# Cross-attention, first batch: a two-tile root, another order of loads, and the turned rows scaled on ScalarE

## The chip, the cores and the metric

The kernel runs on one core of one Trainium2 chip. The metric is the time of one launch on the device, in microseconds (us). The kernel before took 1183.37 us (median of three runs, 1183.1 to 1183.62).

## What is computed

Eight batches of 512 rows with 512 features go through two blocks. The first is a gated cross-attention against a context of the same shape, the second a self-attention with experts. The change touches only the first block, and of it only the first batch.

```python
def _L0_xattn_ref(encoder_hc, decoder_hq, w_sim, b_sim, W_qv, b_qv):
    d = encoder_hc.shape[-1]
    w1, w2, w3 = (w_sim[:d], w_sim[d:2 * d], w_sim[2 * d:])
    Sim = (encoder_hc @ w1)[:, :, None] + (decoder_hq @ w2)[:, None, :] + jnp.einsum('bid,bjd->bij', encoder_hc * w3, decoder_hq) + b_sim[0]
    A = jax.nn.softmax(Sim, axis=2)
    hq_hat = jnp.einsum('bij,bjd->bid', A, decoder_hq)
    Batt = jax.nn.softmax(jnp.max(Sim, axis=2), axis=1)
    hc_bar = jnp.einsum('bi,bid->bd', Batt, encoder_hc)[:, None, :]
    hc_hat = jnp.broadcast_to(hc_bar, encoder_hc.shape)
    feats = jnp.concatenate([encoder_hc, hq_hat, encoder_hc * hq_hat, encoder_hc * hc_hat], axis=-1)
    return feats @ W_qv + b_qv

x = x + jnp.tanh(g_xattn[0]) * _L0_xattn_ref(_layernorm(x, axis=-1), ctx_1024, ...)
x = x + jnp.tanh(g_ffn[0]) * _L0_ffn_ref(_layernorm(x, axis=-1), ...)
```

`_layernorm` subtracts the mean of a row and divides by the root of its variance plus 1e-5. `encoder_hc` is the normalised x, `decoder_hq` the context.

## The kernel before, in words

A batch is four row tiles of 128 rows; its context is held as four tiles of rows (ctx) and four tiles of features (ctx^T, laid out by the host). Every fp32 operand of a product is split in a high part (ScalarE, a copy that rounds, names with `_hi`) and a low part (the rest; VectorE or GpSimd, names with `_lo`), and a product is three passes over four feature tiles, 12 matmuls of 512 columns. The order of work on each engine is written out by hand; semaphores tie the engines together, and each engine works through its own list in order.

What happens in the first batch, before any product can run:

- SyncE (SP) issues the loads in order: four tiles of x (`load_x`), the columns of w_sim (`w_cols`), four tiles of ctx^T (`load_first_ctx_t`), four of ctx (`load_first_ctx`), a weight block `wh_raw`. Then x of batch 1 into the slots of `stage` that the turned rows set free.
- VectorE (DVE) takes the statistics of the four row tiles (`row_stats`, L640), computes 1 over the root of all four variances together in a chain of 17 tiny instructions (`root`, in 14 parts of `mean_rstd`, L47 to L71; each part waits for the one before), and then goes through `first_softmax` (L753 to L798): it normalises the row tiles (L651), takes low parts of ctx^T (`ctx_t_lo`, L253), scales the turned rows with w3 and adds w2 (`first_scaled`, L681: four instructions of 128x128 from PSUM into `tmp`), takes the low part of the scaled rows (`first_scaled_lo`, L689), finds row maxima of the scores (`row_max`, L729), inverts the sums (L734) and takes low parts of the turned probabilities (`probs_lo`, L744).
- TensorE (PE) fills time with transposes of the identity (`fill`, L953), turns the normalised rows (`turn_e`, four transposes, L964), computes the scores of one row tile at a time (`scores`, L946; row tile t waits for `es_lo` t+1), sums the rows against w1 (`first_dots`, L970), turns the probabilities (`turn_a`, L999) and then, when the low part of the last turned probabilities is there, computes the attended context (`attend`, L946 into ps_h). From there on it goes on with the products of the batch (`feats`) and with batch 1.
- ScalarE (ACT) takes the high parts (`ctx_t_hi` and `ctx_hi` and `weights_hi`, all L249; `first_scaled_hi`, L472), copies the turned rows from PSUM (`copy_e`, L466), computes the exponentials (`softmax_exp`, L504), normalises them (`normalise`, L513) and takes the high part of the turned probabilities (`probs_hi`, L509).
- GpSimd (POOL) takes the low parts of ctx and of the weights; it waits for the low parts of the third and fourth scaled row tile first.

Row tile t has t as its number in what follows, so the scores of tile 0 are the first.

Of the kernel before, what the change touches and what calls it, by code (L numbers as in the profile page):

```python
# [24 lines left out]
ALU = mybir.AluOpType  # L25
# [87 lines left out]
def cross_attention(nc, block, both, x, ctx, ctx_t, g_xattn, w_sim, w_sim_cols, b_sim, w_qv, b_qv, x1, w_vsd, wq, wk):  # L113
# [7 lines left out]
    with ExitStack() as mem:  # L121
# [78 lines left out]
        c_lo = sem("c_lo")  # L200
        stats_done = sem("stats_done")
        newton = sem("newton")
        all_stats_done = sem("all_stats_done")
        x1_newton = sem("x1_newton")
        e_ready = sem("e_ready")
# [72 lines left out]

        @block.sync
        def _(sp):  # L280
            def load_x(b, first=False, second=False):
                for t in range(NT):
                    if second:

                        sp.wait_ge(et_ps, t + 1)
                    elif not first:

                        sp.wait_ge(c_lo, b * NT - NT + t + 1)
                    sp.dma_start(stage[:, t, :], of(x_dram, b)[:, t, :]).then_inc(slot_loaded[t], 16)
# [11 lines left out]
                    sp.wait_ge(ct_lo, b * ND + t + 1)  # L301
                    sp.dma_start(stage[:, t, :], of(c_dram, b)[:, t, :]).then_inc(slot_loaded[t], 16)

            def load_first_ctx_t():
                for k in range(ND):
                    sp.dma_start(x_sb[:, k, :], of(ct_dram, 0)[:, k, :]).then_inc(ct0_loaded[k], 16)

            def load_first_ctx():
# [22 lines left out]
                sp.wait_ge(x1_stats_done, (b + 1) * NT)  # L331
                load_residual(b + 1)

            load_x(0, True)
            sp.dma_start(w_cols[:], w_sim_cols).then_inc(cols_loaded, 16)
            load_first_ctx_t()
            load_first_ctx()
            sp.dma_start(wh_raw[:], w_blocks[1]).then_inc(wh_loaded, 16)
            load_x(1, second=True)
# [122 lines left out]
        def _(act):  # L462
            def copy_e(b, t, first=False):
# [2 lines left out]
                act.activation(e_t[:, :, t * P:(t + 1) * P], first_turned[t] if first else turned_e[t],  # L466
                               ACT.Copy).then_inc(et_copied, 1)

            def first_scaled_hi(t):
                cols = slice(t * P, (t + 1) * P)  # L470
                act.wait_ge(es_ready, t + 1)
                act.activation(es_t2[:, 0, :, cols], tmp[:, :, cols], ACT.Copy).then_inc(es_hi, 1)  # L472
# [99 lines left out]
                ctx_hi(b, False)  # L572

            def first_softmax():
                for k in range(ND):
                    ctx_t_hi(0, k, True)
                first_scaled_hi(0)
                copy_e(0, 0, True)
                ctx_hi(0, True)
                first_scaled_hi(1)  # L580
                copy_e(0, 1, True)
                weights_hi(wh, wh_raw, wh_loaded, (0,))
                softmax_exp(0, 0)
                first_scaled_hi(2)
                normalise(0, 0)
                copy_e(0, 2, True)
                softmax_exp(0, 1)
                probs_hi(0, 0)
                first_scaled_hi(3)
                normalise(0, 1)  # L590
                copy_e(0, 3, True)
                weights_hi(wh, wh_raw, wh_loaded, (1,))
                probs_hi(0, 1)
                softmax_exp(0, 2)
                normalise(0, 2)
                weights_hi(wh, wh_raw, wh_loaded, (2, 3))
                probs_hi(0, 2)
                softmax_exp(0, 3)
                normalise(0, 3)
# [34 lines left out]
        def _(dve):  # L634
# [7 lines left out]
            def root(b, part):  # L642
                if part == 0:
                    dve.wait_ge(stats_done, b * NT + NT)
                mean_rstd(dve, part, stats[:], D, mean[:], work[:], rstd[:], newton, b * ROOT_STEPS)

            def normalise_x(b, t):
                if t == 0:

                    dve.wait_ge(newton, b * ROOT_STEPS + ROOT_STEPS)  # L650
                dve.tensor_scalar(e_sb[:, t, :], e_sb[:, t, :], mean[:, t:t + 1], rstd[:, t:t + 1],  # L651
                                  ALU.subtract, ALU.mult).then_inc(e_ready, 1)
# [19 lines left out]
            def scaled_e_lo(b, k):  # L672
                dve.wait_ge(es_hi, b * ND + k + 1)
                take_lo(dve, es_t2, k, tmp).then_inc(es_lo, 1)

            def first_scaled(t):
                dve.wait_ge(et_ps, t + 1)
                if t == 0:
                    dve.wait_ge(cols_loaded, 16)
                for k in range(ND):  # L680
                    last = dve.tensor_scalar(tmp[:, k, t * P:(t + 1) * P], first_turned[t][:, k, :], w3_col[:, k:k + 1],  # L681
                                             w2_col[:, k:k + 1], ALU.mult, ALU.add)
                last.then_inc(es_ready, 1)

            def first_scaled_lo(t):
                cols = slice(t * P, (t + 1) * P)
# [65 lines left out]

            def first_softmax():  # L753

                normalise_x(0, 0)
                normalise_x(0, 1)
                ctx_t_lo(0, 0, True)
                first_scaled(0)
                ctx_t_lo(0, 1, True)
                normalise_x(0, 2)  # L760
                first_scaled_lo(0)
                ctx_t_lo(0, 2, True)
                ctx_t_lo(0, 3, True)
                first_scaled(1)
                normalise_x(0, 3)
                first_scaled_lo(1)
                row_max(0, 0)
                first_scaled(2)
                invert(0, 0)
                first_scaled_lo(2)  # L770
                row_max(0, 1)
                first_scaled(3)
                invert(0, 1)
                probs_lo(0, 0)
                first_scaled_lo(3)
                row_max(0, 2)
                row_stats(1, 0)
                invert(0, 2)
                probs_lo(0, 1)
                row_stats(1, 1)  # L780
                row_max(0, 3)
                row_stats(1, 2)
                invert(0, 3)
                probs_lo(0, 2)
                row_stats(1, 3)
                for part in range(5):
                    root(1, part)
                probs_lo(0, 3)
                first_dots()
                row_totals(0)  # L790
                for part in range(5, ROOT_PARTS):
                    root(1, part)

                first_row_lo(1, 1)
                first_row_lo(2, 2)
# [101 lines left out]
                dve.tensor_scalar(all_stats[:, bass.ds(b * NT, NT), :], x1_stats[:], 1.0, None,  # L897
                                  ALU.mult).then_inc(all_stats_done, 1)

            for t in range(NT):  # L900
                row_stats(0, t, True)
            for part in range(ROOT_PARTS):
                root(0, part)
            first_softmax()
            attended(0, True, True)
            with dve.Fori(0, B - 2) as b:
# [28 lines left out]
        def _(pe):  # L935
# [130 lines left out]
            def softmax(b, first):  # L1066


                scores(b, 0, first)
                if first:  # L1070
                    turn_e(0, 2, True)
                    turn_e(0, 3, True)
                if not first:
                    scores(b, 1, False)
                    feats(b - 1, *LAST_FEATS[0])
# [11 lines left out]
                for t in range(NT):  # L1087
                    if t + 1 < NT:
                        scores(b, t + 1, True)
                    if t == 0:  # L1090
                        first_dots(0)
                    if t == NT - 1:
                        fill(3)
                        first_dots(1)
                        fill(3)
                        first_dots(2)
                        fill(3)
                    turn_a(b, t, True)
                fill(6)
                first_dots(NT - 1)  # L1100

            pe.wait_ge(stats_done, 3)
            fill(18)
            turn_e(0, 0, True)
            turn_e(0, 1, True)
            fill(12)
            softmax(0, True)
            first_feats(0, True, True)
            softmax(1, False)
# [1163 lines left out]
```

## Time and profile before

| | us |
|---|---|
| median of three runs | 1183.37 |
| the profiled execution's own time | 1182.84 |
| its span, first to last instruction | 1181.0 |
| PE busy | 1166.8 (99%) |
| DVE busy | 831.3 (70%) |
| ACT busy | 647.1 (55%) |
| POOL busy | 657.4 (56%) |

The granted TensorE clock is in the highest tenth in all 40 slices of the page. The 1.84 us between the span and the time of that execution lie before the first and behind the last instruction. A row of the timeline gives the start, the length of the merged row, engine, line, operation, what is written from what, and how many instructions it merges; in brackets how long the engine was idle before it and what ended that. Instructions of DVE and ACT overlap a little: a 128x512 copy on ACT lasts 0.62 us, and the next begins 0.52 us after it.

### The profile page before, as it was taken

The page shows a single profiled execution, that of the slowest core. Times are in us where ns is not written, and L with a number is a line of the kernel's source. Part 1 is how long each engine was busy: PE and PEld are TensorE (multiplying, and loading weights), DVE is VectorE, ACT ScalarE, POOL GpSimd, SP SyncE. Part 2 cuts the span into 40 slices and gives each one's busy share as a digit, 9 for nine tenths or more (in the row PEclk, how much of TensorE's full clock was granted, in tenths as well). Part 3 has the DMA queues.
Part 4 walks back from the last instruction along what each step waited for, and adds up shares of the span by engine and source line. Part 5 has one row for each costly group of instructions (what it writes and reads, how often), then busy time and mean ns, then how long its engine had stood idle before and what let it go on. Part 6 is the DMA issues. An engine that isn't in the chain of part 4 may idle for free.

```text
span 1181.0 us, 19684 instructions
## 1 busy us (share of the span) xinstructions
PE 1166.8 (99%) x6377; PEld 910.1 (77%) x6377; DVE 831.3 (70%) x1518; ACT 647.1 (55%) x1444; POOL 657.4 (56%) x476
## 2 busy tenths in 40 slices
PE   7999999999999999999999999999999999999998
PEld 6888888888888888877767777677677777777765
DVE  7888787878787857465675765666666765765868
ACT  6534343434343534477656666556657666665654
POOL 2625242424242425449298297397397396495594
PEclk9999999999999999999999999999999999999999
DMA  5441413131323224401003002002002011010020
GB/s 198 142 134 45 134 55 123 63 114 68 110 77 101 80 62 150 153 11 37 1 1 107 0 18 89 0 27 80 0 36 71 0 60 46 0 71 0 0 72 36
DMA packets 40749, 75.92 MB, mean 64 GB/s; under 512 B 3728, under 2 KB 4240, under 8 KB 40720
## 3 DMA queue, kind: packets, MB, share of 16 engines
q1 hardware_dynamic: 40720, 75.55, 19.1%
q8 instruction: 16, 0.26, 0.1%
q14 instruction: 13, 0.11, 0.0%
HBM read 58.76 MB, written 16.78 MB: 64 GB/s over the span
## 4 chain that ended last, share of the span: by engine, by line
PE 90%; DVE 4%; issue 1%; ACT 0%; POOL 0%; DVEq 0%
PE ps_f L946 21%; PE ps_r L2019 14%; PE ps_o L2089 9%; PE ps_s L2076 8%; PE ps_s L2068 8%; PE ps_s L946 6%; PE ps_h L946 6%; PE ps_r L2028 6%; PE ps_r L2052 4%; PE ps_r L2034 1%; PE ps_r L2010 1%; PE ps_r L2042 1%; DVE nmax L1692 1%; PE ps_t L999 1%; PE ps_h L999 1%
## 5 line engine op out<-in xcount | busy, mean ns | idle before, releaser
L1692 DVE TENSOR_REDUCE nmax<-ps_s 128x1 f32<-128x512 f32 x256 | 158.7, 682 | 112.9 <-PE ps_s L2068 111.9
L1523 ACT ACTIVATE tmp<-ps_s,nmax 128x512 f32<-128x512 f32 x256 | 172.7, 687 | 94.0 <-DVE nmax L1692 94.0
L1466 POOL TENSOR_TENSOR z<-z,z_tmp 128x1280 f32<-128x1280 f32 x35 | 102.9, 2939 | 166.3 <-DVE z_tmp L1706 164.0
L1448 POOL TENSOR_TENSOR spare<-xv,pick 128x512 f32<-128x512 f32 x160 | 169.4, 1059 | 35.6 <-DVE pick L1801 22.7
L1454 POOL TENSOR_TENSOR spare<-spare 128x512 f32<-128x512 f32 x128 | 181.5, 1418 | 10.0
L1532 ACT ACTIVATE pt<-ps_s 128x512 f32<-128x512 f32 x256 | 132.1, 612 | 10.5 <-PE ps_s L2076 10.5
L2076 PE MATMUL ps_s<-ident,tmp 128*128 128x128 f32 x1024 | 122.3, 273 | 0.0
L2076 PEld LDWEIGHTS ps_s<-ident,tmp 128*128 128x128 f32 x1024 | 115.4, 140 | 8.6 <-issue 1.6
L2089 PE MATMUL ps_o<-pt,spare 128*64 128x512 f32 x496 | 113.3, 598 | 0.0
L253 POOL TENSOR_TENSOR e_t<-e_t 128x512 fp32r<-128x512 f32 x28 | 35.4, 1300 | 139.7 <-ACT e_t L493 139.7
L2068 PE MATMUL ps_s<-k,q 64*128 64x512 f32 x768 | 107.0, 409 | 0.1
L2068 PEld LDWEIGHTS ps_s<-k,q 64*128 64x128 f32 x768 | 66.9, 184 | 47.1 <-issue 33.9
L253 POOL TENSOR_TENSOR c<-stage,c 128x512 fp32r<-128x512 f32 x28 | 42.3, 1542 | 97.7 <-ACT c L249 97.7
L2019 PE MATMUL ps_r<-es_t,c_t 128*128 128x512 f32 x384 | 96.2, 399 | 0.0
L2019 PE MATMUL ps_r<-es_t,wk 128*128 128x512 f32 x384 | 95.1, 396 | 0.0
L946 PE MATMUL ps_s<-c_t,es_t 128*128 128x512 f32 x384 | 92.5, 392 | 1.2 <-DVE es_t L689 1.1
L946 PE MATMUL ps_f<-wec,e_t 128*128 128x512 f32 x384 | 92.1, 392 | 0.0
L946 PE MATMUL ps_f<-weh,eh_t 128*128 128x512 f32 x384 | 91.9, 391 | 0.0
L946 PE MATMUL ps_f<-wh,h_t 128*128 128x512 f32 x384 | 91.1, 390 | 0.3 <-DVE x_sb L888 0.3
L946 PE MATMUL ps_h<-es_t,c 128*128 128x512 f32 x384 | 88.7, 390 | 0.0
L946 PEld LDWEIGHTS ps_f<-wh,h_t 128*128 128x128 f32 x384 | 72.0, 188 | 15.6 <-DVE x_sb L888 0.7
L946 PEld LDWEIGHTS ps_s<-c_t,es_t 128*128 128x128 f32 x384 | 71.3, 188 | 16.1 <-DVE es_t L689 1.6
(234 smaller groups left out, 2116.7 us busy)
## 6 DMA issues: line engine op xcount, KB each, us to landing
stage<-in_x SPq DMA_DIRECT2D x32, 256.0 KB, 3.2
x_sb<-in_x SPq DMA_DIRECT2D x8, 1024.0 KB, 5.1
x_dram<-x_sb SPq DMA_DIRECT2D x32, 256.0 KB, 3.3
stage<-x_dram SPq DMA_DIRECT2D x8, 1024.0 KB, 5.7
x_sb<-x_dram SPq DMA_DIRECT2D x8, 1024.0 KB, 5.6
out_dram<-x_sb SPq DMA_DIRECT2D x32, 256.0 KB, 2.0
stage<-in_ctx_t SPq DMA_DIRECT2D x28, 256.0 KB, 2.8
stage<-in_ctx SPq DMA_DIRECT2D x28, 256.0 KB, 2.7
```

The lines of the kernel that those rows point to most:

```text
L253: return eng.tensor_tensor(pair[:, 1, k, :], operand[:, k, :], pair[:, 0, k, :].bitcast(F32), ALU.subtract)
L946: last = pe.matmul(out, left(l, k), right(r, k), start=start and n == 1, stop=stop and n == ND * len(PASSES))
L1448: pool.tensor_tensor(v_tmp[:] if e else acc, xv[:, :, e, :].unsqueeze(2).broadcast_to(shape), pick[:, 0, e, :, 2 * p:2 * p + 2].unsqueeze( ...
L1454: pool.tensor_tensor(acc, acc, v_tmp[:], ALU.add).then_inc(v_steps, 1)
L1466: pool.tensor_tensor(zv, zv, z_tmp[:, h % 2], ALU.add).then_inc(z_pool, 1)
L1523: act.activation(probs[:, n % BANKS, :], ps_s[:, n % BANKS, :], ACT.Exp, bias=nmax[:, n:n + 1], accum_out=den[:, h, t:t + 1]).then_inc(p_e ...
L1532: act.activation(pt[:, h % 4, :, t * P:(t + 1) * P], ps_s[:, n % BANKS, :].rearrange("p (k t) -> p k t", k=NT), ACT.Copy).then_inc(pt_read ...
L1692: dve.tensor_reduce(nmax[:, n:n + 1], ps_s[:, n % BANKS, :], AX_X, ALU.max, negate=True).then_inc(nmax_ready, 1)
L2019: end = pe.matmul(ps, w2[:, l, k, n * P:(n + 1) * P], y_t2[:, r, k, :], start=m == 0, stop=m == len(every) - 1)
L2068: end = pe.matmul(ps_s[:, (n + a) % BANKS, :], q2[head_rows(a), p % 2, l, t * P:(t + 1) * P], k2[head_rows(a), p % 2, r, :], start=m == 0, ...
L2076: end = pe.transpose(ps_s[:, n % BANKS, k * P:(k + 1) * P], probs[:, n % BANKS, k * P:(k + 1) * P], ident[:])
L2089: end = pe.matmul(ps_o[head_rows(a), :], v_acc[:, p, k, a, :], pt[:, p % 2 * 2 + a, k, :], start=k == 0, stop=k == NT - 1)
```

## The change

In `cross_attention`, first batch alone:

- VectorE no longer takes the statistics of all four row tiles before one root. It takes those of tiles 0 and 1, computes their root (`first_root(0, ...)`, a semaphore of its own), normalises both, and then takes the statistics of tiles 2 and 3. Their root's parts are spread between its later work, and `first_normalise(2)` and `(3)` come after the first row maximum.
- SyncE loads x 0 and 1, ctx^T 0 and 1, `w_cols`, x 2 and 3, ctx^T 2 and 3.
- The scaling of the turned rows (`first_scaled`, 16 instructions of 128x128) goes from VectorE to ScalarE, as an activation Identity with a scale and a bias from `w_cols`. The order of ScalarE's `first_softmax` is changed: ctx^T 2 and 3 between the scaled tiles, ctx tile 2 and 3 later, the first weight tile later.
- TensorE turns row tiles 2 and 3 behind the scores of tile 1 and not behind those of tile 0. Its fills begin when the first statistics are done (before: the third), and the second fill is 8 instead of 12.

```diff
-            load_x(0, True)
+            load_first_x((0, 1))
+            load_first_ctx_t((0, 1))
             sp.dma_start(w_cols[:], w_sim_cols).then_inc(cols_loaded, 16)
-            load_first_ctx_t()
+            load_first_x((2, 3))
+            load_first_ctx_t((2, 3))
             load_first_ctx()
...
+            def first_scaled(t):
+                act.wait_ge(et_ps, t + 1)
+                if t == 0:
+                    act.wait_ge(cols_loaded, 16)
+                for k in range(ND):
+                    last = act.activation(tmp[:, k, t * P:(t + 1) * P], first_turned[t][:, k, :], ACT.Identity,
+                                          bias=w2_col[:, k:k + 1], scale=w3_col[:, k:k + 1])
+                last.then_inc(es_ready, 1)
...
             def first_softmax():
-                for k in range(ND):
-                    ctx_t_hi(0, k, True)
+                ctx_t_hi(0, 0, True)
+                ctx_t_hi(0, 1, True)
+                first_scaled(0)
                 first_scaled_hi(0)
+                ctx_t_hi(0, 2, True)
+                first_scaled(1)
+                ctx_t_hi(0, 3, True)
+                first_scaled_hi(1)
                 copy_e(0, 0, True)
-                ctx_hi(0, True)
-                first_scaled_hi(1)
+                ctx_hi(0, True, (0, 1))
+                softmax_exp(0, 0)
                 copy_e(0, 1, True)
-                weights_hi(wh, wh_raw, wh_loaded, (0,))
-                softmax_exp(0, 0)
+                normalise(0, 0)
+                ctx_hi(0, True, (2,))
+                first_scaled(2)
                 first_scaled_hi(2)
-                normalise(0, 0)
+                softmax_exp(0, 1)
+                first_scaled(3)
+                first_scaled_hi(3)
+                probs_hi(0, 0)
+                normalise(0, 1)
                 copy_e(0, 2, True)
-                softmax_exp(0, 1)
-                probs_hi(0, 0)
-                first_scaled_hi(3)
-                normalise(0, 1)
+                ctx_hi(0, True, (3,))
                 copy_e(0, 3, True)
-                weights_hi(wh, wh_raw, wh_loaded, (1,))
+                weights_hi(wh, wh_raw, wh_loaded, (0, 1))
                 probs_hi(0, 1)
                 softmax_exp(0, 2)
...
+            def first_root(half, part):
+                tiles = slice(2 * half, 2 * half + 2)
+                if part == 0:
+                    dve.wait_ge(stats_done, 2 * half + 2)
+                mean_rstd(dve, part, stats[:, tiles, :], D, mean[:, tiles], work[:, :, tiles], rstd[:, tiles],
+                          newton if half else first_newton, 0)
...
-                normalise_x(0, 0)
-                normalise_x(0, 1)
+                row_stats(0, 0, True)
+                row_stats(0, 1, True)
+                for part in range(ROOT_PARTS):
+                    first_root(0, part)
+                first_normalise(0)
+                first_normalise(1)
+                row_stats(0, 2, True)
+                row_stats(0, 3, True)
                 ctx_t_lo(0, 0, True)
-                first_scaled(0)
+                first_scaled_lo(0)
                 ctx_t_lo(0, 1, True)
-                normalise_x(0, 2)
-                first_scaled_lo(0)
+                first_root(1, 0)
+                first_root(1, 1)
                 ctx_t_lo(0, 2, True)
+                first_root(1, 2)
+                first_root(1, 3)
                 ctx_t_lo(0, 3, True)
-                first_scaled(1)
-                normalise_x(0, 3)
                 first_scaled_lo(1)
+                for part in range(4, 9):
+                    first_root(1, part)
                 row_max(0, 0)
-                first_scaled(2)
+                for part in range(9, 12):
+                    first_root(1, part)
                 invert(0, 0)
+                for part in range(12, ROOT_PARTS):
+                    first_root(1, part)
+                first_normalise(2)
+                first_normalise(3)
+                row_max(0, 1)
                 first_scaled_lo(2)
-                row_max(0, 1)
-                first_scaled(3)
                 invert(0, 1)
                 probs_lo(0, 0)
                 first_scaled_lo(3)
...
                 scores(b, 0, first)
-                if first:
-                    turn_e(0, 2, True)
-                    turn_e(0, 3, True)
...
                     if t == 0:
+                        turn_e(0, 2, True)
+                        turn_e(0, 3, True)
                         first_dots(0)
...
-            pe.wait_ge(stats_done, 3)
+            pe.wait_ge(stats_done, 1)
             fill(18)
             turn_e(0, 0, True)
             turn_e(0, 1, True)
-            fill(12)
+            fill(8)
```

## Rows read from the trace of the kernel before

**Rows 1.** Who PE waited for, 0 to 36 us (total, times, longest)
```profile
PE ps_b L953 <- DVE stats L640: 6.3, 1, 6.3
PE ps_s L946 <- DVE es_t L689: 1.1, 1, 1.1
```
**Rows 2.** The same view, 36 us to the end
```profile
PE ps_r L2156 <- DVE z_t L1886: 1.0, 1, 1.0
...
PE ps_f L946 <- DVE x_sb L888: 0.3, 1, 0.3
```
**Rows 3.** Timeline of PE, 0 to 34 us
```profile
6.31 4.07 PE L953 MATMUL ps_b<-ident 128*128 128x128 f32 x18 [6.31 <-DVE stats L640]
10.46 1.11 PE L964 MATMUL ps_t<-ident,stage 128*128 128x128 f32 x4
...
12.12 1.47 PE L953 MATMUL ps_b<-ident 128*128 128x128 f32 x12
14.69 3.02 PE L946 MATMUL ps_s<-c_t,es_t 128*128 128x512 f32 x12 [1.10 <-DVE es_t L689]
...
18.64 3.04 PE L946 MATMUL ps_s<-c_t,es_t 128*128 128x512 f32 x12
21.51 0.95 PE L970 MATMUL ps_b<-w_cols,e_t 128*128 128x1 f32 x8
22.32 0.64 PE L999 MATMUL ps_t<-ident,a_sb 128*128 128x128 f32 x4
22.71 3.00 PE L946 MATMUL ps_s<-c_t,es_t 128*128 128x512 f32 x12
...
33.91 3.01 PE L946 MATMUL ps_h<-es_t,c 128*128 128x512 f32 x12
```
**Rows 4.** Timeline of DVE, 0 to 20 us
```profile
3.52 1.32 DVE L640 BATCH_NORM_STATS2 stats<-stage 128x6 f32<-128x512 f32 x2 [3.52 <-DMA stage<-in_x]
5.47 1.35 DVE L640 BATCH_NORM_STATS2 stats<-stage 128x6 f32<-128x512 f32 x2 [0.63 <-DMA stage<-in_x]
...
9.66 0.16 DVE L71 SCALAR_TENSOR_TENSOR rstd<-work,rstd 128x4 f32<-128x4 f32 x1
9.86 1.00 DVE L651 TENSOR_SCALAR stage<-stage,mean,rstd 128x512 f32<-128x512 f32 x2
...
11.61 1.36 DVE L681 TENSOR_SCALAR tmp<-ps_t,w_cols 128x128 f32<-128x128 f32 x4 [0.15 <-PE ps_t L964]
...
14.55 1.28 DVE L253 TENSOR_TENSOR c_t<-x_sb,c_t 128x512 fp32r<-128x512 f32 x2
...
18.50 0.68 DVE L729 TENSOR_REDUCE nmax<-ps_s 128x1 f32<-128x512 f32 x1
```
**Rows 5.** Timeline of ACT, 0 to 34 us
```profile
6.82 0.63 ACT L249 ACTIVATE c_t<-x_sb 128x512 fp32r<-128x512 f32 x1 [4.79 <-DMA x_sb<-in_ctx_t]
...
14.03 2.18 ACT L249 ACTIVATE c<-spare 128x512 fp32r<-128x512 f32 x4
...
26.19 0.60 ACT L509 ACTIVATE es_t<-ps_h 128x512 fp32r<-128x512 f32 x1
26.68 0.69 ACT L504 ACTIVATE a_sb<-ps_s,nmax 128x512 f32<-128x512 f32 x1
27.25 0.20 ACT L504 ACTIVATION_READ_ACCUMULATOR a_sb<-ps_s,nmax 128x1 f32 x1
```
**Rows 6.** Groups of ACT by form: count, busy us, mean ns, idle before
```profile
L1514 ACT ACTIVATE stage<-stage,norm 128x512 f32<-128x512 f32 x28 | 21.4, 822 | 0.0
...
L1561 ACT ACTIVATE xv<-ps_r 128x320 f32<-128x320 f32 x32 | 14.6, 458 | 0.0
...
L1558 ACT ACTIVATE logits<-ps_r 128x80 f32<-128x80 f32 x32 | 8.2, 255 | 29.8 <-PE ps_r L2028 20.3 <-POOL spare L1454 9.5
...
L249 ACT ACTIVATE c<-spare 128x512 fp32r<-128x512 f32 x4 | 2.2, 617 | 0.0
...
L1623 ACT ACTIVATE z<-z 128x128 f32<-128x128 f32 x2 | 0.6, 310 | 4.4 <-DVE z L1879 4.4
```

More of the change, by code:

```diff
@@ L202, in cross_attention @@
         newton = sem("newton")
+        first_newton = sem("first_newton")
         all_stats_done = sem("all_stats_done")
@@ L280, in _, with load_x @@
         def _(sp):
-            def load_x(b, first=False, second=False):
+            def load_x(b, second=False):
                 for t in range(NT):
@@ L285, in load_x @@
                         sp.wait_ge(et_ps, t + 1)
-                    elif not first:
+                    else:
                         sp.wait_ge(c_lo, b * NT - NT + t + 1)
@@ L302, in load_ctx, with load_first_x, load_first_ctx_t @@
                     sp.dma_start(stage[:, t, :], of(c_dram, b)[:, t, :]).then_inc(slot_loaded[t], 16)
-            def load_first_ctx_t():
-                for k in range(ND):
+            def load_first_x(tiles):
+                for t in tiles:
+                    sp.dma_start(stage[:, t, :], of(x_dram, 0)[:, t, :]).then_inc(slot_loaded[t], 16)
+            def load_first_ctx_t(tiles):
+                for k in tiles:
                     sp.dma_start(x_sb[:, k, :], of(ct_dram, 0)[:, k, :]).then_inc(ct0_loaded[k], 16)
@@ L574, in first_softmax @@
             def first_softmax():
-                for k in range(ND):
-                    ctx_t_hi(0, k, True)
+                ctx_t_hi(0, 0, True)
+                ctx_t_hi(0, 1, True)
+                first_scaled(0)
                 first_scaled_hi(0)
+                ctx_t_hi(0, 2, True)
+                first_scaled(1)
+                ctx_t_hi(0, 3, True)
+                first_scaled_hi(1)
                 copy_e(0, 0, True)
-                ctx_hi(0, True)
-                first_scaled_hi(1)
+                ctx_hi(0, True, (0, 1))
+                softmax_exp(0, 0)
                 copy_e(0, 1, True)
-                weights_hi(wh, wh_raw, wh_loaded, (0,))
-                softmax_exp(0, 0)
+                normalise(0, 0)
+                ctx_hi(0, True, (2,))
+                first_scaled(2)
                 first_scaled_hi(2)
-                normalise(0, 0)
+                softmax_exp(0, 1)
[3 more added lines that the diff above has]
+                normalise(0, 1)
                 copy_e(0, 2, True)
-                softmax_exp(0, 1)
-                probs_hi(0, 0)
-                first_scaled_hi(3)
-                normalise(0, 1)
+                ctx_hi(0, True, (3,))
                 copy_e(0, 3, True)
-                weights_hi(wh, wh_raw, wh_loaded, (1,))
+                weights_hi(wh, wh_raw, wh_loaded, (0, 1))
                 probs_hi(0, 1)
@@ L645, in root, with first_normalise @@
                 mean_rstd(dve, part, stats[:], D, mean[:], work[:], rstd[:], newton, b * ROOT_STEPS)
+            def first_root(half, part):
[4 more added lines that the diff above has]
+                          newton if half else first_newton, 0)
+            def first_normalise(t):
+                dve.wait_ge(newton if t >= 2 else first_newton, ROOT_STEPS)
+                dve.tensor_scalar(e_sb[:, t, :], e_sb[:, t, :], mean[:, t:t + 1], rstd[:, t:t + 1],
+                                  ALU.subtract, ALU.mult).then_inc(e_ready, 1)
             def normalise_x(b, t):
@@ L674, in scaled_e_lo @@
                 take_lo(dve, es_t2, k, tmp).then_inc(es_lo, 1)
[L676 to L683, printed above, removed]
             def first_scaled_lo(t):
@@ L898, in keep_stats @@
                                   ALU.mult).then_inc(all_stats_done, 1)
[L900 to L903, printed above, removed]
             first_softmax()
```

## The prediction, made before the changed kernel ran

> **What bounds the kernel now.** PE is busy for 99% of the span, so I read first where it waits. Up to 36 us it waits twice: 6.3 us for the first statistics, and 1.1 us for the low part of scaled tile 0 [rows 1]. Behind 36 us the longest single wait is 1.0 us, at the very end, and in the first batch it is 0.3 us [rows 2]; none is for a DMA. So whatever moves the start of the first `attend` product (33.91 [rows 3]) moves the end of the kernel by as much: the loads behind it and all other engines hang on PE's progress and shift along. The question is only when `attend` starts. For that I read the four timelines side by side and asked at each step what came last.
>
> The way there has a first part bound by VectorE (statistics, the root, normalising, turning, scaling, low part: scores of tile 0 at 14.69 [rows 3, 4]) and a second in which PE, DVE and ACT alternate (scores, maximum, exponential, normalising, turning, high, low). PE covers its gaps there with fills and dots.
>
> **What things cost.** I use lengths and start-to-start distances from the rows. DVE: the statistics of the last tile end at 6.82, the root ends at 9.82, 3.0 us later; it is a chain in which each part waits 0.2 us for the one before, so that two columns instead of four save nothing. Normalising is 0.54 us, the second 0.46 later; a low part 0.69, the next 0.6 later; a maximum 0.68 [rows 4]. PE: four transposes take 1.11 us at first and about 0.6 later; 12 transposes of the second fill take 1.47 us where 18 of the first take 4.07, so early ones are at half pace. Scores take 3.0 us, the next work starts 2.85 after them; dots 0.8, turning the probabilities 0.4 to 0.6 [rows 3]. ACT: a 128x512 copy 0.63, the next 0.52 to 0.54 later (four in 2.18); a high part from PSUM 0.49 to the next [rows 5]; an exponential 0.77 with the reading of its accumulator [rows 5]. A semaphore between two engines costs about 0.04.
>
> The one price the trace doesn't show is the moved piece: an activation of 128x128 from PSUM with both a scale and a bias from memory. Copies of 128x80 and 128x320 from PSUM take 0.255 and 0.458 us, so 128 columns lie at 0.29; a 128x128 copy from SBUF takes 0.310. Two operands from memory make a 128x512 activation 0.822 instead of 0.617, 0.2 more [rows 6]; overlap takes 0.1 off between neighbours [rows 5]. That is 0.39; with PSUM's copies a little below the means I take 0.37 to the next and 0.47 for the last. Lower bound 0.20 (the operands cost nothing in a row of short ones), upper 0.42. DVE's own piece is 0.32 ((1.36 - 0.40) / 3, with 0.40 for the last of the four [rows 4]), so ACT is not quicker at this. The Trainium skill (ScalarE: Activation LUTs, What ACT_TABLE_LOAD costs) gives 186 ns plus 0.833 ns per column, 93 ns more for each pointer operand and 93 ns of overlap, which is 0.386 us a piece. By that price the sum below would be about 0.2 us more, 1185.8. Its Rules for kernel authors ask for VectorE for multiplications and additions, since it is up to three times as fast per element in bf16; in fp32 the rows show 0.32 against 0.37, so that rule would make the move dearer than the rows do.
>
> **The front part.** x 0 and 1 keep the first two places of SP's queue, and statistics 0 and 1 end at 4.84. ctx^T 0 and 1 take the places of x 2 and 3 (there by 5.5 and 6.2 [rows 4]), x 2 and 3 those of ctx^T 0 and 1 (the first is there at 6.82 [rows 5]); DVE asks for x 2 at 8.8 and for x 3 at 9.4. All are wanted later than they land, so the loads' order costs and gains nothing by itself. Root from 4.9, normalised tile 0 from 7.9 to 8.46 (9.86 before). PE's fills start at 4.25 and end at 8.35, still covering. Turned at half pace 8.52 to 9.63. ACT scales in 1.58 (to 11.25) and takes the high part to 11.92, DVE the low part to 12.65, and scores 0 start at 12.71, 1.98 us ahead.
>
> They don't keep it. In ACT's queue ctx^T 2 (to 12.46), the scaling of tile 1 (12.37 to 13.95) and ctx^T 3 (to 14.48) come first, so the fourth low part of ctx^T ends at 15.29 and scores 0 at 16.2 (17.71 before): 1.5 ahead. Low part of tile 1 at 15.90, scores 1 from 16.1 to 19.1, 2.5 ahead, since two turns no longer lie before them.
>
> **The second root.** DVE does its parts between other work. The root costs 2.9 us more on DVE and 16 scaling pieces of 0.32 (5.1 us) leave it, but the chain's parts now lie before work that is wanted: five parts (1.0 us) before maximum 0, which starts at 16.70 instead of 18.50. Exponential 17.42 to 18.20; the reciprocal; two parts; tiles 2 and 3 normalised from 18.72 to 19.72. In before they were turned between scores 0 and 1, 17.7 to 18.6 [rows 3]. PE turns them 19.32 to 20.4, then dots, then the probabilities of tile 0 (21.0, 22.32 before). PE's cover is thinner here: it waits 0.4 before the turn.
>
> **Where the gain goes.** Now ACT must scale tile 2: 19.96 to 21.54, high part to 22.21, low part to 22.94, scores 2 at 23.00, against 22.71: 0.3 late. From 19.96 on ACT has no gap. Start to start: high part of tile 2 ends its slot at 22.12, exponential 1 0.68, scaling tile 3 1.48 and 0.14 of waiting for its own end, high part 0.54, probabilities 0 high 0.49, normalise 1 0.61: 26.06. Then copy 0.48, ctx 3 0.52, copy 0.48, two weight tiles 1.04, probabilities 1 high 0.49: exponential 2 starts at 29.07. In before it started at 26.68 [rows 5]. Scores 2 ended at 26.0, the maximum at 27.5, so they aren't what it waits for. What is new in ACT's queue in this stretch is two scalings (3.2 us), one ctx tile and one weight tile (0.52 each), all done earlier or elsewhere in before. From exponential 2 on, the order is the same as before; 33.91 - 26.68 = 7.23 us to `attend`, 7.19 by my own walk. So `attend` starts at 36.26.
>
> As a check of the bookkeeping, the same durations walked through the order of before put `attend` at 33.99 where the trace has 33.91. Against the walk's own 33.99 the change costs 36.26 - 33.99 = +2.27 us. GpSimd and the weight loads have room: the last high part that they wait for, ctx 3's, ends at 27.2, nine us before `attend`.
>
> **The sum.** 1182.84 + 2.27 = 1185.11 for the profiled execution; the median of the runs is 0.53 above that execution, so 1185.6. A price p of a piece enters about 12 times, 0.6 us for 0.05: at 0.20 `attend` is at 34.22 (+0.2, 1183.6), at 0.25 34.82 (+0.8), at 0.42 36.98 (+3.0, 1186.4). The first turn at full pace would take 0.5 off. The measurement can tell about 0.2%, 2.37 us, from no change; the forecast lies just inside.
>
> **Rivals.**
> - *ACT's queue as worked out* (+1.8 to +2.8, 1185.2 to 1186.2): 0.58. For it: every other term stands in the trace.
> - *Short pieces are cheaper in a row* (0.20 to 0.33, +0.2 to +1.8, 1183.6 to 1185.1): 0.17. ACT's smallest pieces never stand four in a row in the trace.
> - *The change does what it says*: the 2 us of the front survive, 1181.4: 0.05. ACT would have to absorb 16 pieces for nothing; even at 0.12 a piece `attend` would be at 33.26, only 0.7 ahead.
> - *Dearer pieces or a queue that waits more often* (+2.8 to +3.9, up to 1187.3): 0.10. Each piece reads a bank PE wrote just before; a further 0.07 each is 0.9 us.
> - *Slower, by the clock*: PE now idles 1.6 us before scores 2 and 1.1 before turning probabilities 2, where before its longest idle stretch since the start of the fills was 1.1 [rows 1]. If its clock fell to the lower level before scores 2, at half pace [rows 3] they would end at 28.9, exponential 2 would be 0.4 late, and scores 3 would end at 35 instead of 29.9, which puts exponential 3 some 3.7 late: +6, about 1189.5. It decides if the granted clock or the pace of the matmuls falls anywhere between 20 and 30 us. Against it: PE is still busy most of that stretch. 0.10.
>
> **How the numbers follow.** Slower by over 0.2%: the clock, the dearer pieces, and the upper part of the likeliest case (0.22 of 0.58): 0.42. Within 0.2%: the rest of it and the cheaper pieces: 0.53. Faster: 0.05. The range leaves out the gain and the clock, 0.15 together: 1183.3 to 1187.3.
>
> **What would show it.** Right: scores 0 near 12.7, maximum 0 near 16.7, tiles 2 and 3 turned near 19.3, scores 2 near 23, exponential 2 near 29, `attend` near 36.3; ACT without idle from 20 to 29; scaling groups of four lasting 1.5 to 1.6. Wrong: a group of 1.0 to 1.2; `attend` later than 34 for another reason than ACT (PE's pace); or a different time with `attend` where I say, which would mean that the shift isn't carried to the end.

## The result, and the profile after

The changed kernel takes 1184.44 us (median of 20 runs, 1183.81 to 1188.88), the kernel before 1182.82 (20 runs beside it). That is 1.62 us more. The means lie a little further apart, since two of the twenty executions took 1188.8: their ratio is 1.0017 with a 95% interval of 1.0011 to 1.0024. So it is slower, by less than the 0.2% that I had set as the bound. Forecast were 2.27 us more. The profiled execution took 1184.12 us, its span is 1182.3.

The page of after, span and engines:

```profile
span 1182.3 us, 19693 instructions
...
PE 1168.3 (99%) x6373; PEld 909.9 (77%) x6373; DVE 827.5 (70%) x1519; ACT 652.0 (55%) x1460; POOL 657.2 (56%) x476
```

DVE has lost 3.8 us of busy time and ACT gained 4.9. The direction is that of the moved pieces (four groups of 1.36 us on DVE [rows 4], four of 1.50 on ACT) less the second root on DVE; the sizes don't add up to the tenth. The timeline of PE of after, first batch (start, length, line, how many; in brackets the idle time before):

```profile
4.09 4.07 PE L988 MATMUL ps_b<-ident 128*128 128x128 f32 x18 [4.09 <-DVE stats L663]
8.20 0.81 PE L999 MATMUL ps_t<-ident,stage 128*128 128x128 f32 x4
...
12.07 6.24 PE L981 MATMUL ps_s<-c_t,es_t 128*128 128x512 f32 x24 [1.75 <-DVE es_t L716]
18.53 0.66 PE L999 MATMUL ps_f<-ident,stage 128*128 128x128 f32 x4 [0.22 <-DVE stage L680]
...
22.24 4.58 PE L981 MATMUL ps_s<-c_t,es_t 128*128 128x512 f32 x12 [1.32 <-DVE es_t L716]
...
27.02 3.02 PE L981 MATMUL ps_s<-c_t,es_t 128*128 128x512 f32 x12
...
35.29 3.04 PE L981 MATMUL ps_h<-es_t,c 128*128 128x512 f32 x12
```

Read against [rows 3]: scores 0 start 2.62 us earlier than before, tiles 2 and 3 are turned at 18.53, scores 2 start only 0.47 earlier and take 4.58 us instead of 3.00, scores 3 start 1.1 later than before (25.91 there), and `attend` starts at 35.29 instead of 33.91: 1.38 us late. Span and `attend` moved together (1.3 and 1.38), so nothing behind it gave anything back. The row of scores 3 in before:

```profile
25.91 3.02 PE L946 MATMUL ps_s<-c_t,es_t 128*128 128x512 f32 x12
```

And ACT of after in the same stretch:

```profile
16.66 0.69 ACT L520 ACTIVATE a_sb<-ps_s,nmax 128x512 f32<-128x512 f32 x1 [0.98 <-DVE nmax L756]
...
19.23 1.50 ACT L481 ACTIVATE tmp<-ps_f,w_cols 128x128 f32<-128x128 f32 x4 [0.17 <-PE ps_f L999]
...
21.96 1.49 ACT L481 ACTIVATE tmp<-ps_h,w_cols 128x128 f32<-128x128 f32 x4
...
28.10 0.70 ACT L520 ACTIVATE a_sb<-ps_s,nmax 128x512 f32<-128x512 f32 x1
```

From 19.23 on no row of ACT has an idle time until exponential 2 has started at 28.10 (26.68 before [rows 5]). Four pieces last 1.50 us, one 0.455 by the median, so they follow each other by (1.50 - 0.455) / 3 = 0.348 us.

The 4.58 us of scores 2 are the clock. The busy time of PE in stretches of 1 us, with the granted clock behind it (1.00 is the level of 2.4 GHz, 0.50 that of 1.2):

```profile
20.00:21.00 1.00, 0.92 (x8) 1.00 0.75 270
21.00:22.00 1.00, 0.00 (x0) 1.00 0.74 254
22.00:23.00 1.00, 0.76 (x2) 0.61 0.26 90
23.00:24.00 1.00, 1.00 (x4) 0.50 0.78 273
24.00:25.00 1.00, 1.00 (x4) 0.50 0.40 154
25.00:26.00 1.00, 1.00 (x5) 0.69 0.04 16
```

That is the rival "slower, by the clock", in the place where I had put it. It did not cost what I had priced: scores 2 ended at 26.82 and the maximum of their rows at 27.55, before ACT was free for exponential 2 at 28.10. The turned probabilities of tile 1, which stand behind scores 2 in PE's list, were there at 27.26, and ACT came to them at 27.62:

```profile
26.66 0.60 PE L1034 MATMUL ps_h<-ident,a_sb 128*128 128x128 f32 x4
```
```profile
27.62 0.60 ACT L525 ACTIVATE es_t<-ps_h 128x512 fp32r<-128x512 f32 x1
```

So there were two limits less than half a us apart (0.36), ACT's queue and the slowed scores, and one profile doesn't tell which one to remove. The experiments do.

### The profile page after: what moved, and what is told of

Its sections match the earlier page's. It is cut to its first block, busy times and chain, and to the rows that moved or that the text cites. A ratio compares the mean times of both kernels' runs of the same rounds, so it can differ in the third digit from the quotient of the medians.

```text
span 1182.3 us, 19693 instructions
## 1 busy us (share of the span) xinstructions
PE 1168.3 (99%) x6373; PEld 909.9 (77%) x6373; DVE 827.5 (70%) x1519; ACT 652.0 (55%) x1460; POOL 657.2 (56%) x476
## 4 chain that ended last, share of the span: by engine, by line
PE 93%; DVE 1%; issue 1%; ACT 0%; POOL 0%; DVEq 0%
PE ps_f L981 21%; PE ps_r L2053 15%; PE ps_o L2123 9%; PE ps_s L2110 9%; PE ps_s L2102 8%; PE ps_s L981 6%; PE ps_h L981 6%; PE ps_r L2062 6%; PE ps_r L2086 4%; PE ps_r L2068 1%; PE ps_r L2044 1%; PE ps_r L2076 1%; PE ps_t L1034 1%; PE ps_h L1034 1%; PE ps_r L2190 1%
```

## The experiments

Each kernel was timed in five rounds beside the kernel before on the same chip; the differences below are medians against that one. Of the kernel after this difference is +1.62. Of the front each profiled execution has its own share: scores 0 start at 12.07 us in the kernel after and at 12.25 to 12.68 in its variants with the same front. So what lies behind the front is best read from the start of scores 0 to the start of `attend`, 23.22 us in the kernel after.

**Tiles 2 and 3 scaled on VectorE again.**

```diff
 ScalarE, first_softmax
-                first_scaled(2)
                 first_scaled_hi(2)
                 softmax_exp(0, 1)
-                first_scaled(3)
                 first_scaled_hi(3)
 VectorE, first_softmax
                 row_max(0, 1)
+                first_scaled(2)
+                first_scaled(3)
                 first_scaled_lo(2)
```

> The kernel after, with the scaling of row tiles 2 and 3 given back to VectorE (both behind the maximum of scores 1, before the low part of tile 2); ScalarE keeps tiles 0 and 1. Theory Q (ScalarE's queue from 19 to 28 us is what costs): exponential 2 starts near 26.9 instead of 28.1, attend starts 1.2 to 1.3 us before that of the kernel after (35.29), near 34.0, and the whole kernel is about 1.3 us faster than the kernel after, within 0.4 us of the kernel before. Rival T (the late turn of tiles 2 and 3, behind the second root, is what costs): attend stays at 35.3, since the tiles are turned no earlier. Rival C (the half clock in scores 2): attend stays near 35.3 if the clock falls again in scores 2, and moves only where it doesn't.

Measured 1185.13 us, +2.02: no gain at all. Nine of its eleven executions lie at 1184.9 to 1186.1, with a mean granted clock of 0.999 or less. The other two took 1183.20 and 1183.37, with a clock of 1.000: they are where theory Q had put the kernel, within 0.4 us of the one before. The timelines of PE and of ACT of the profiled execution (1185.14) show what stood in the way:

```profile
23.29 4.60 PE L990 MATMUL ps_s<-c_t,es_t 128*128 128x512 f32 x12 [1.81 <-DVE es_t L723]
...
36.08 3.01 PE L990 MATMUL ps_h<-es_t,c 128*128 128x512 f32 x12
```
```profile
28.37 0.60 ACT L525 ACTIVATE es_t<-ps_h 128x512 fp32r<-128x512 f32 x1 [1.44 <-PE ps_h L1043]
```

ACT now idles 1.44 us for PE, which turns the probabilities of tile 1 behind scores 2: its queue is no longer the limit, the slowed scores 2 are. The granted clock fell to 0.50 behind an idle stretch of 1.81 us.

**The same, with PE kept busy.** Twelve more transposes of the identity before scores 0, fourteen before scores 2.

```diff
             turn_e(0, 1, True)
-            fill(8)
+            fill(20)
 ...
                     turn_a(b, t, True)
+                    if t == 0:
+                        fill(14)
```

> The run with tiles 2 and 3 scaled on VectorE (median 1185.13, two of its eleven executions at 1183.3), with 12 more transposes before scores 0 and 14 before scores 2, so that PE has no idle stretch over 0.4 us there. Theory Q and C together (the queue is one limit, the half clock in scores 2 a second at nearly the same place): scores 2 take 3.0 us, attend near 34.2, median near 1183.3. If the queue alone mattered there would be no change against 1185.13; if the clock falls elsewhere instead, attend is again 1.5 us or more later.

Measured 1183.06, +0.13, all eleven executions between 1182.88 and 1183.32. PE:

```profile
22.92 3.06 PE L990 MATMUL ps_s<-c_t,es_t 128*128 128x512 f32 x12 [0.28 <-DVE es_t L723]
...
34.17 3.06 PE L990 MATMUL ps_h<-es_t,c 128*128 128x512 f32 x12
```

Scores 2 are at full pace and `attend` starts at 34.17, 1.9 us before the run without the fills; 0.4 of that is the front (scores 0 at 12.25 and at 12.63). The granted clock is 1.000 in all eleven executions. Both theories hold, one behind the other.

**The kernel after with such fills**, its scaling untouched (12 before scores 2 instead of 14):

> The kernel after, with 12 more transposes before scores 0 and 12 before scores 2, nothing else. With tiles 2 and 3 on VectorE such fills brought 1185.13 to 1183.06. Theory: here ScalarE's queue is the limit and the half clock in scores 2 lay in its shadow, so attend stays at 35.2 to 35.6 and the median at 1184.1 to 1184.6; scores 2 take 3.0 us. If the clock was what made the kernel after slower, this gains 1.5 us.

```profile
22.82 3.01 PE L981 MATMUL ps_s<-c_t,es_t 128*128 128x512 f32 x12
...
35.88 3.02 PE L981 MATMUL ps_h<-es_t,c 128*128 128x512 f32 x12
```

Scores 2 take 3.01 us instead of 4.58, and it gains nothing: 1184.94, +1.92, above the 1184.1 to 1184.6 that I had expected. `attend` starts at 35.88, 0.3 later than expected, but scores 0 start 0.6 later too, at 12.65. In the kernel after the slowed scores lie in the shadow of ACT's queue; here that queue alone is the limit. With the front taken out, the four kernels stand so (scores 0 to `attend` in us, and the difference of the medians):

| scaling of tiles 2 and 3 | without the fills | with them |
|---|---|---|
| on ScalarE | 23.22, +1.62 | 23.23, +1.92 |
| on VectorE | 23.45, +2.02 | 21.92, +0.13 |

Either step alone gains nothing, both together gain 1.3 us behind the front and 1.5 in the medians. Four of the eleven executions of the kernel with fills took 1186.3 to 1189.0, with a granted clock of 0.995 to 0.998, and two of the twenty of the kernel after took 1188.8, with 0.995. The next run shows what a fall at another place costs.

**Fills before scores 2 alone** (`fill(12)` behind the turned probabilities of tile 0).

> The kernel after, with 12 more transposes of the identity between the turned probabilities of tile 0 and scores 2, 1.3 us of work in the gap ahead of which the granted clock fell to 0.50. Rival C: scores 2 take 3.0 instead of 4.6 us and the kernel is up to 1.5 us faster than the kernel after. Theory Q: scores 2 take 3.0 us, but exponential 2 stays at 28.1 and attend at 35.3, since ScalarE gets to it no sooner; the time is that of the kernel after within 0.3 us. If the rare executions of the kernel after with 4.4 us more come from this clock, there is none here.

Measured 1186.08, +2.97, where at most 0.3 from the kernel after was expected. The eleven executions fall in three groups: four at 1184.3 to 1185.0 (clock 1.000), five at 1186.0 to 1186.5, two at 1188.9 and 1189.0 (clock 0.995). The profiled one took 1186.04 and belongs to the middle group. In it scores 2 took 3.02 us, but the clock fell at another place. PE's busy time and the granted clock:

```profile
32.00:33.00 1.00, 1.00 (x12) 1.00 1.05 408
33.00:34.00 1.00, 1.00 (x7) 0.56 0.87 318
34.00:35.00 1.00, 1.00 (x7) 0.50 0.93 340
```
```profile
37.10 2.99 PE L981 MATMUL ps_h<-es_t,c 128*128 128x512 f32 x12
```

From 31 us on PE is never idle here; it works through fills and the one-column dots, behind an idle stretch of 0.91 us at 30. That work slowed down and `attend` came at 37.10, 24.55 us behind scores 0 instead of 23.2. So a fall of the clock here costs 1.3 us, where the one in scores 2 of the kernel after cost nothing, because PE's own list is the limit there: ACT waits 1.56 us for the turned probabilities of tile 3. The executions near 1188.8 are another matter: 4.4 us above the median, over three times the size of this. Their low granted clock is on record, but where it fell in them isn't known, since none of them was profiled.

**The doubled pieces.** ScalarE does the eight pieces of tiles 2 and 3 twice.

```diff
                 last.then_inc(es_ready, 1)
+                if t >= 2:
+                    for k in range(ND):
+                        act.activation(h_t2[:, 1, k, t * P:(t + 1) * P], first_turned[t][:, k, :], ACT.Identity,
+                                       bias=w2_col[:, k:k + 1], scale=w3_col[:, k:k + 1])
```

> The kernel after, in which ScalarE does each of the eight scaling pieces of tiles 2 and 3 a second time, into a tile that is not in use yet. Theory Q: 8 pieces of 0.348 us in a queue without idle cost at most 2.8 us, and by my walk 2.5 us (0.3 of it lies in a gap): attend near 37.8, kernel 2.5 us slower than the kernel after. Rivals T and C: the pieces lie in ScalarE's slack and cost under 1 us.

Measured 1187.04, +3.93, 2.3 us more than the kernel after:

```profile
24.00 4.37 PE L985 MATMUL ps_s<-c_t,es_t 128*128 128x512 f32 x12 [2.56 <-DVE es_t L720]
...
38.30 3.04 PE L985 MATMUL ps_h<-es_t,c 128*128 128x512 f32 x12 [0.15 <-DVE es_t L775]
```

`attend` starts 3.0 us later than in the kernel after, 0.5 of it the front: 25.72 us behind scores 0, 2.5 more. That is the walk's number; eight pieces of 0.348 are 2.8. What ACT does there is paid nearly in full.

**ScalarE's scaling alone**, in the kernel before: `first_scaled(t)` right ahead of each `first_scaled_hi(t)` on ScalarE, none on VectorE.

> The kernel before, with one part of the change alone: ScalarE does the scaling of all four turned row tiles, each right ahead of the high part of that tile; one root for four tiles, old loads, tiles 2 and 3 turned behind scores 0. Theory Q: the walk puts exponential 2 at 29.3 instead of 26.7 and attend at 36.4 instead of 33.9, +2.6 us, and this is worse than the whole change. Rival T: little or nothing is lost, since no turn is late here. Rival C: nothing, unless the clock falls here too.

Measured 1185.29, +2.36. PE:

```profile
28.67 0.66 PE L999 MATMUL ps_h<-ident,a_sb 128*128 128x128 f32 x4 [1.33 <-ACT a_sb L522]
...
37.17 3.01 PE L946 MATMUL ps_h<-es_t,c 128*128 128x512 f32 x12
```

Here PE waits 1.33 us for the normalised probabilities of tile 1, at full clock (1.000 in all eleven executions). So the move to ScalarE costs by itself, with no late turn and no clock. The profiled execution took 1185.95, the longest of the eleven: its first statistics end 0.64 us later than in [rows 3], so of the 3.26 us by which `attend` is late 2.6 are the change, as expected.

**The two-tile root and the late turns, without the scaling on ScalarE**: the kernel after with VectorE scaling all four tiles. The new order of the loads and of ScalarE's list stays in it.

> The kernel after with VectorE scaling all four tiles, so the two-tile root and the late turns alone. Theory Q by the walk: VectorE now has the second root and the scaling (5.1 us) in one queue ahead of maximum 0, scores 0 start at 13.2 to 13.5, maximum 0 at 19.2 instead of 16.0, attend at 38.5, about 3 us later than in the kernel after. So the two-tile root needs the scaling off VectorE for tiles 0 and 1. A theory in which ScalarE's scaling alone is to blame expects this to be faster than the kernel after.

Measured 1188.37, +5.44, 3.8 more than the whole change (five executions):

```profile
13.47 4.61 PE L981 MATMUL ps_s<-c_t,es_t 128*128 128x512 f32 x12 [2.99 <-DVE es_t L712]
18.76 3.01 PE L981 MATMUL ps_s<-c_t,es_t 128*128 128x512 f32 x12 [0.67 <-DVE es_t L712]
...
38.92 3.02 PE L981 MATMUL ps_h<-es_t,c 128*128 128x512 f32 x12
```

Scores 0 start at 13.47, 1.2 us earlier than before, but scores 1 at 18.76 and `attend` at 38.92. The second root and the scaling don't fit into VectorE's list together. The clock fell here too, in scores 0, but they ended at 18.08 and VectorE came to their maximum only at 19.48, so that isn't what costs. The parts of the change aren't additive: +2.36 and +5.44 alone, +1.62 together.

**The old order of the loads** in the kernel after:

> The kernel after, with the loads in the order of before (x 0 to 3, the columns of w_sim, ctx^T 0 to 3). Every theory: ctx^T 0 and 1 are there at 6.8 and 8.2 us and their high parts done by 8.9, before the first scaling at 9.05, so nothing moves: within 0.3 us of the kernel after. It also tells whether the first x tile, there at 3.25 us in the profile of after and at 3.52 in that of before, owes that to the order of the loads (then 3.5 here, and up to 0.25 us slower) or to the execution.

Measured 1184.89, +1.78, against +1.62: nothing.

```profile
12.68 6.29 PE L979 MATMUL ps_s<-c_t,es_t 128*128 128x512 f32 x24 [1.29 <-DVE es_t L714]
...
22.86 3.02 PE L979 MATMUL ps_s<-c_t,es_t 128*128 128x512 f32 x12 [1.32 <-DVE es_t L714]
...
35.93 3.02 PE L979 MATMUL ps_h<-es_t,c 128*128 128x512 f32 x12 [0.15 <-DVE es_t L769]
```

The first x tile came at 3.58 us here, but at 3.60 in the run with the fill before scores 2, which has the new order, so that is the execution's. In this execution, with x as late as in [rows 4], the first turn at half pace (1.12 us) and no fall of the clock, `attend` starts at 35.93, 2.0 us later than in before and 23.25 behind scores 0. It has no slowed scores 2 and is no shorter for it, which is the table's first row once more, without any fill.

**Another order for the same work.** If the limit is who waits for whom, it should be possible to keep the 2 us of the front. Scaling: ScalarE tiles 0 and 1, VectorE 2 and 3. Of the fourteen parts of the second root on VectorE, the first stands alone, five stand in the idle time before the low part of tile 0 and four one by one behind long instructions, where their wait is hidden; the last four follow as a chain. PE turns tile 2 right behind scores 0 and tile 3 behind scores 1, and has eight transposes more before scores 0; ScalarE's tiles of ctx and of the weights are spread over its list. These steps were not tried one by one. The core of it, as the new lists have it (excerpt, not a diff):

```python
# VectorE, first_softmax, behind the first root (half 1 is the second root)
first_root(1, 0)
ctx_t_lo(0, 0, True)
for part in range(1, 6):
    first_root(1, part)
first_scaled_lo(0)
first_root(1, 6)
ctx_t_lo(0, 1, True)
first_root(1, 7)
ctx_t_lo(0, 2, True)
...
for part in range(10, 14):
    first_root(1, part)
first_normalise(2)
first_scaled_lo(1)
row_max(0, 0)
first_scaled(2)
first_normalise(3)
...
# TensorE, first_softmax
scores(0, 0, True)
first_dots(0)
turn_e(0, 2, True)
scores(0, 1, True)
turn_e(0, 3, True)
turn_a(0, 0, True)
scores(0, 2, True)
scores(0, 3, True)
```

> Another order for the same work, in which nothing waits long: two-tile root, ScalarE scales tiles 0 and 1, VectorE 2 and 3; the parts of the second root stand one at a time behind 0.6 us instructions and in VectorE's idle time before the low part of tile 0, so that tiles 2 and 3 are turned right behind scores 0; ScalarE's ctx and weight tiles are spread into its gaps; more fills before scores 0. By the walk: tile 2 turned at 16.0 to 16.3 (18.5 in the kernel after), exponential 2 at 24.2 to 24.5, attend at 31.2 to 31.5, 2.5 us ahead of the kernel before: about 1180.4. If the clock falls in scores 2 or 3, 1 to 2 us of that are gone.

Measured 1181.74, -1.19 by the medians, half of what I expected. Six of the eleven executions took 1181.4 to 1181.7, the other five 1182.8 to 1183.5, and the interval of the ratio, 0.9986 to 1.0004, still holds no change. The profiled execution, 1183.02, is one of the five. In it the chain went as planned up to exponential 2 (24.21), then this, on DVE, POOL and PE:

```profile
28.75 0.63 DVE L47 TENSOR_TENSOR work<-stats 128x8 f32<-128x8 f32 x1
29.30 1.30 DVE L48 TENSOR_TENSOR work<-stats 128x4 f32<-128x4 f32 x1
```
```profile
26.83 3.75 POOL L254 TENSOR_TENSOR wh<-spare,wh 128x512 fp32r<-128x512 f32 x3
```
```profile
32.79 4.49 PE L992 MATMUL ps_h<-es_t,c 128*128 128x512 f32 x12 [1.51 <-DVE es_t L781]
```
```profile
32.00:33.00 1.00, 0.21 (x1) 0.79 0.94 365
33.00:34.00 1.00, 1.00 (x3) 0.50 1.02 393
```

Two instructions that take 0.17 and 0.15 us elsewhere took 0.63 and 1.30, while GpSimd worked on its weight tiles, and the second ended as GpSimd did (30.60 and 30.58). They are ahead of the last two low parts in VectorE's list; PE idled 1.5 us for them, and then the clock fell and `attend` itself took 4.49 us. The six shorter executions have a mean granted clock of 1.000, so as far as a mean can tell this fall is missing in them.

**GpSimd's third weight tile behind the root of batch 1.**

```diff
-            weight_lo(wh, wh_raw, 0, (0, 1, 2))
+            weight_lo(wh, wh_raw, 0, (0, 1))
             pool.wait_ge(newton, 2 * ROOT_STEPS)
-            weight_lo(wh, wh_raw, 0, (3,))
+            weight_lo(wh, wh_raw, 0, (2, 3))
```

> The reordered kernel (median 1181.74), in which two instructions of 128x8 and 128x4 on VectorE took 0.63 and 1.30 us instead of 0.17 and 0.15 while GpSimd worked on its third weight tile; the slow one ended with GpSimd's (30.60 and 30.58 us). Here GpSimd does that weight tile behind its wait for the root of batch 1, with the fourth. Theory P (VectorE's small instructions are held up by GpSimd's): both take 0.17 us again, the last low part starts near 30.6 instead of 32.1, attend near 31.4 instead of 32.8, and PE no longer idles 1.5 us before it, so the clock has less reason to fall: about 1180.4 to 1180.8. If the two were slow for another reason they stay so, and the time is 1181.7.

Measured 1181.35 (1181.09 to 1181.78), -1.67, a ratio of 0.9987 with an interval of 0.9978 to 0.9996: faster than both kernels, and all eleven executions lie below the shortest of the kernel before beside it (1182.08). It is less than the 1180.4 to 1180.8 that I had expected. DVE and PE:

```profile
28.83 0.62 DVE L47 TENSOR_TENSOR work<-stats 128x8 f32<-128x8 f32 x1
29.37 0.15 DVE L48 TENSOR_TENSOR work<-stats 128x4 f32<-128x4 f32 x1
```
```profile
20.15 6.07 PE L992 MATMUL ps_s<-c_t,es_t 128*128 128x512 f32 x24
...
31.72 3.02 PE L992 MATMUL ps_h<-es_t,c 128*128 128x512 f32 x12 [0.35 <-DVE es_t L781]
```

The second instruction is down to 0.15; the first, which I had expected at 0.17, still takes 0.62 and ends at 29.45, when GpSimd's last tile before its wait ends (29.42). PE idles 0.35 us instead of 1.51, and the granted clock is 1.000 in all eleven executions. `attend` starts at 31.72, 2.2 us before that of [rows 3]. Of these, 1.7 reach the end: PE now waits 0.7 us for `x_sb` at the residual, where it waited 0.3 before [rows 2]. The trace shows what precedes it: two VectorE instructions at 48.45 take 2.43 us together, where they took 1.40 in before, while GpSimd is at an instruction from 48.21 to 49.67. That GpSimd is there because the weight tile was pushed into its later work is argued, not tried.

## Why the prediction was right, and where it was off

**The bound.** Right. `attend` is the place through which everything goes: in the kernel after it starts 1.38 us late and the span is 1.3 longer; in the doubled run 4.4 late, 3.9 in the medians. In the last run a later wait took some of it back, and in the reordered kernel's profile `attend` itself was slowed by the clock.

**The time.** The forecast of 1185.6 stood on a median of 1183.37 from three runs. Twenty runs of the same kernel gave 1182.82, so 0.55 of the 1.2 us by which 1185.6 is above the measured 1184.44 is that base, and 0.65 is the change itself (2.27 against 1.62).

**The price of a piece.** Taken at 0.37, which was my estimate and no row, and measured at 0.348. Entering twelve times, that is -0.26 us. (By the same twelve, the upper price of 0.42 puts `attend` at 36.86, not at 36.98.) The estimate from the figures of the Trainium skill was 0.386 (ScalarE: Activation LUTs, What ACT_TABLE_LOAD costs); the measurement decides, and both were close.

**The front.** Scores 0 were forecast for 12.71 and start at 12.07: x came at 3.25 instead of 3.5 in that execution, and the first turn took 0.81 instead of 1.11. Neither belongs to the change. The forecast less the 0.26 is 2.01; the run with the old loads, where both are as I had assumed them, has 2.02 (35.93 - 33.91). The profile of after has 1.38, and 2.01 less 0.27 for x and 0.3 for the turn is 1.44. So the number came out nearer to zero in part by the luck of one execution.

**The second root and the late turns.** Forecast at 19.3, measured 18.5, 0.6 of that from the front. Maximum 0 at 15.94, five parts of the root ahead of it, as worked out.

**Where the gain goes.** Right: ACT's queue from scaling tile 2 to exponential 2, 8.87 us without a gap where I had 9.11. Doubling pieces in it costs 2.3 to 3.0 us, taking PE's slow scores away gains nothing, and taking two scalings out of it gains 1.3 us behind the front, 1.8 by the medians, as soon as the clock doesn't fall.

**The step that failed** is the price of the rival of the clock. I gave it 0.10 and +6 us, with the clock low for scores 2 and 3. It fell in the profile of after, in the place named, but scores 2 lost 1.58 us by it and not 2.9: it was up again before scores 3, which took 3.02. For exponential 2 I had taken the later of the two limits, 0.4 late; nearly all of the 6 us was scores 3 at half pace, which didn't happen, and what was left ACT's queue hid. Its chance of 0.10 was too low as well: the mean granted clock is below 1.000 in 12 of the kernel's 20 executions. Hidden isn't gone: with the queue shortened the same fall costs the whole gain.

**The rival "the change does what it says"** is refuted for this change. But the front's 2 us can be kept by another order, with the root's parts in gaps and each engine scaling two tiles: the last run starts `attend` 2.2 us earlier than before.

## What to carry over

When work is moved from a busy engine to an idle one, walk the other engine's list from the point where the moved work is wanted to the next thing that others wait for; ACT is idle for 45% of the span and has no gap at all in the 9 us that count. A chain of tiny dependent instructions costs its 0.2 us waits only when it stands alone: with one part behind each long instruction it takes 0.07 us a part (in the reordered kernel a part starts at 12.24 us and the next long instruction at 12.31). And where two limits lie within half a us of each other, removing one shows next to nothing; try both together before the idea is dropped.

## What the runs showed of the hardware

TensorE's granted clock fell to 0.50 behind idle stretches of 1.3 to 3.0 us (1.32, 1.51, 1.81, 2.56 and 2.99 in five profiles), and not behind others as long: 1.75 us before scores 0 in the kernel after left it at 1.00, as did 1.32 us before scores 2 in the run with the old loads. In one run it fell at 33 us while PE was busy without a break with fills and one-column dots. What decides between these cases is open: with 26 transposes more in the gaps it stayed up in all eleven executions of one kernel, and with 24 more it fell in four of eleven of another.

The first transposes of a launch are slow although the view shows the full clock. In the kernel before 18 of them take 4.07 us and 12 later ones 1.47 [rows 3], and the granted clock reads 1.00 in each us from 6 to 13. So a pace read from the rows says more there than the clock's column.

A tiny two-input instruction on VectorE can be held for as long as GpSimd is in a tile of its own: 0.17 became 0.63 and 0.15 became 1.30 us, each ending with GpSimd's. The Trainium skill says that GpSimd's SBUF interfaces are shared with VectorE, with contention for VectorE's instructions in a 2-port mode or with two SBUF inputs (GPSIMD Engine Reference, Specifications). Both instructions have two SBUF inputs, and moving GpSimd's tile brought the second back to 0.15, so the runs agree. The kernel before has it on larger ones: two low parts of 128x512 at 55.05 us take 2.39 together while GpSimd is busy from 55.21 to 60.29, where two at 14.55 take 1.28 [rows 4].
